# Spreading reciprocal softmax totals on TensorE: one fp32 product against two rounded products of a high and a low part

## The reference, cut to what matters

```python
scores = scores * total_effect
scores = jnp.where(allow, scores, NEG)
attn = jax.nn.softmax(scores, axis=-1)
out = jnp.einsum('bhqk,bhkd->bhqd', attn, v)
```

## Time and profile before

| what | value |
|---|---|
| time before, median of 3 runs | 1689.13 us (1682.05 to 1694.72) |
| time of the profiled execution | 1691.98 us |
| its span, first to last instruction | 1689.0 us |
| its mean granted TensorE clock | 0.953 |
| busy: PE, PEld, DVE, ACT, POOL | 1506.9, 1251.6, 1122.4, 1023.1, 157.9 us |

### The profile page before, as it was taken

How to read it: one execution, slowest core, us unless ns; L and a number is a source line. 1 busy time by engine, 2 the same in 40 slices (tenths; PEclk the granted TensorE clock), 3 DMA queues, 4 the chain that set the end, 5 groups by cost and what they waited for, 6 DMA issues and landing times.

```text
span 1689.0 us, 36801 instructions
## 1 busy us (share of the span) xinstructions
PE 1506.9 (89%) x13056; PEld 1251.6 (74%) x13056; DVE 1122.4 (66%) x3828; ACT 1023.1 (61%) x2674; POOL 157.9 (9%) x107
## 2 busy tenths in 40 slices
PE   4374879999998999999998999999999999988986
PEld 3353668887887888778887878778787878777874
DVE  6576785867766676757857676775857676673221
ACT  1485766676666577666766667666756667674221
POOL 6323110100000010100000010100001010000000
PEclk9786979999998999999999999999999999999998
DMA  5555324656565475646565475656557465566875
GB/s 187 194 187 182 125 101 162 237 177 224 176 212 170 172 251 172 230 170 216 190 207 191 157 244 175 225 177 207 194 178 243 156 234 189 199 224 232 292 270 191
DMA packets 81243, 334.54 MB, mean 198 GB/s; under 512 B 10256, under 2 KB 10256, under 8 KB 64272
## 3 DMA queue, kind: packets, MB, share of 16 engines
q1 hardware_dynamic: 81040, 331.92, 57.3%
HBM read 306.72 MB, written 25.17 MB: 196 GB/s over the span
## 4 chain that ended last, share of the span: by engine, by line
PE 65%; DVE 15%; DMA 8%; issue 5%; ACT 3%; POOL 1%; SPq 1%; DVEq 0%; POOLq 0%; ACTq 0%
PE bank L200 19%; PE bank L201 17%; PE bank L202 17%; PE bank L384 5%; DMA out<-rows 4%; PE bank L398 3%; DVE w_sb L938 3%; DMA w_ring<-w_split 3%; DVE w_sb L950 2%; DVE w_sb L961 2%; PE bank L418 1%; DVE s_sb L926 1%; PE bank L408 1%; DVE c_lo L889 1%; DMA w_split<-w_ring 1%
## 5 line engine op out<-in xcount | busy, mean ns | idle before, releaser
L200 PE MATMUL bank<-xt_hi,w_ring 128*128 128x256 f32 x1024 | 298.4, 291 | 1.9 <-ACT h_sb L721 1.9
L201 PE MATMUL bank<-xt_lo,w_ring 128*128 128x256 f32 x1024 | 291.2, 284 | 0.0
L202 PE MATMUL bank<-xt_hi,w_ring 128*128 128x256 f32 x1024 | 290.8, 284 | 0.0
L200 PE MATMUL bank<-w_ring,h_hi 128*128 128x512 f32 x512 | 219.0, 428 | 23.3 <-DMA w_ring<-w_split 14.7
L721 ACT ACTIVATE h_sb<-bank,b_col 128x256 f32<-128x256 f32 x256 | 106.9, 468 | 212.4 <-DVE h_lo L1027 110.1
L201 PE MATMUL bank<-w_ring,h_hi 128*128 128x512 f32 x512 | 206.4, 403 | 0.0
L384 PE MATMUL bank<-qk_sb 32*32 32x256 f32 (+7 forms) x4096 | 174.3, 298 | 35.8 <-DVE m L926 35.4
L662 ACT ACTIVATE p_sb<-w_sb,nm 128x32 f32<-128x32 f32 (+7 forms) x512 | 206.1, 411 | 0.0
L202 PE MATMUL bank<-w_ring,h_lo 128*128 128x512 f32 x512 | 205.8, 402 | 0.0
L200 PEld LDWEIGHTS bank<-xt_hi,w_ring 128*128 128x128 f32 x1024 | 196.8, 192 | 11.8 <-issue 7.2
L201 PEld LDWEIGHTS bank<-xt_lo,w_ring 128*128 128x128 f32 x1024 | 196.9, 192 | 1.9
(11 more groups left out here) (120 smaller groups left out, 3018.8 us busy)
## 6 DMA issues: line engine op xcount, KB each, us to landing
w_ring<-w_split SPq DMA_DIRECT2D x128, 1024.0 KB, 4.9
w_ring<-w_split SPq DMA_DIRECT2D x256, 512.0 KB, 4.1
w_split<-w_ring SPq DMA_DIRECT2D x32, 512.0 KB, 3.9
x_raw<-x_t SPq DMA_DIRECT2D x16, 512.0 KB, 5.6
c_raw<-ctx_t SPq DMA_DIRECT2D x16, 512.0 KB, 6.2
u_sb<-x_rows SPq DMA_DIRECT2D x16, 512.0 KB, 5.4
ring_raw<-w SPq DMA_DIRECT2D x32, 256.0 KB, 3.0
out<-rows SPq DMA_DIRECT2D x16, 512.0 KB, 6.1
```

What stands on the lines that cost most here:

```text
L200: nc.tensor.matmul(dst, a_hi, b_hi, start=start, stop=False)
L201: nc.tensor.matmul(dst, a_hi, b_lo, start=False, stop=False)
L202: return nc.tensor.matmul(dst, a_lo, b_hi, start=False, stop=stop)
```

## The change

The constant `head_ones_r` is a float32r copy of `head_ones`, made by POOL in its chain of constants. `totals` now makes three more values from the reciprocals: a rounded high part by a copy (128 x 8), a low part by a subtraction (128 x 8), each behind a wait for the last, and one multiplication with `delta` for both parts together, 128 x 512 in place of 128 x 256. `attend` makes two float32r products of 256 columns that add up, in place of one plain fp32 product of 256 columns. Everything else stays as it is.

```diff
+        head_ones_r = tensor("head_ones_r", [P, P], F32R)
...
-        zi_wide = tensor("zi_wide", [P, NB, R])
+        zi_pair = tensor("zi_pair", [P, 2, NB], F32R)
+        zi_wide = tensor("zi_wide", [P, 2, NB, R], F32R)
...
-                nc.tensor.matmul(av_bank[:, S:2 * S], head_ones[:], zi_wide[:].rearrange("p b r -> p (b r)"),
-                                 start=True, stop=True, skip_group_check=True)
+
+                for part in range(2):
+                    nc.tensor.matmul(av_bank[:, S:2 * S], head_ones_r[:], zi_wide[:, part].rearrange("p b r -> p (b r)"),
+                                     start=part == 0, stop=part == 1, skip_group_check=True)
...
                 nc.vector.reciprocal(z2[:, c], z2[:, c]).then_inc(zi2_ok, 1)
-                dve.wait_ge(zi2_ok, NQ * i + c + 1)
+                dve.wait_ge(zi2_ok, 3 * (NQ * i + c) + 1)
+                nc.vector.tensor_copy(zi_pair[:, 0], z2[:, c]).then_inc(zi2_ok, 1)
+                dve.wait_ge(zi2_ok, 3 * (NQ * i + c) + 2)
+                nc.vector.tensor_tensor(zi_pair[:, 1], z2[:, c], zi_pair[:, 0].bitcast(F32),
+                                        ALU.subtract).then_inc(zi2_ok, 1)
+                dve.wait_ge(zi2_ok, 3 * (NQ * i + c) + 3)
                 if c > 0 or not first(i):
                     dve.wait_ge(av_mm, NQ * i + c)
-                nc.vector.tensor_tensor(zi_wide[:], z2[:, c].unsqueeze(2).broadcast_to([P, NB, R]),
-                                        delta[:].unsqueeze(1).broadcast_to([P, NB, R]), ALU.mult).then_inc(wide_ok, 1)
+                parts = zi_pair[:].bitcast(F32).rearrange("p n b -> p (n b)")
+                nc.vector.tensor_tensor(zi_wide[:].rearrange("p n b r -> p (n b) r"),
+                                        parts.unsqueeze(2).broadcast_to([P, 2 * NB, R]),
+                                        delta[:].unsqueeze(1).broadcast_to([P, 2 * NB, R]), ALU.mult).then_inc(wide_ok, 1)
...
+            then(nc.gpsimd.tensor_copy(head_ones_r[:], head_ones[:]))
...
-CONSTS = 4 + 9 + 1 + 12 + 1 + 8
+CONSTS = 4 + 9 + 1 + 12 + 1 + 1 + 8
```

## The result

| | median us (range, runs) | ratio to before, 95% interval |
|---|---|---|
| before | 1685.99 (1679.25 to 1694.72, 17) | |
| after | 1691.19 (1688.96 to 1702.89, 17) | 1.0043 [1.0025, 1.0061] |

A forecast was written before the change was run, and what follows sets the result against it. A PE stretch and a stretch from the store through DVE to `rows_low(0)`, in series, were taken as the bound; 0.35 + 1.5 + 6.8 - 7.8 + 0 = +0.9 us gave a median of 1690 us, range 1679 to 1699.

The forecast's parts named there:

- Two stretches in series: Each turn: a PE stretch, then 24 us from the store to `rows_low(0)` in which PE has room to spare.
- s and d: Per call, s is PE's saving at `attend`, 0.20 us; d is DVE's added time in `totals`, 0.73 us.
- Quarter 3 pays, the others don't: DVE's added time delays `hidden_low(7)` and PE in quarter 3, 6.8 us; quarters 0 to 2 are covered, at nothing.
- eight full and five partial charges: Quarter 3, in front of `add_hidden(7)`: 8 x 0.73 + 5 x 0.2 = 6.8 us.
- POOL's copy at the start: Filling stage: the 128 x 128 copy joins the chain of constants that `inputs_high(0)` waits for, 0.35 us.
- Where the PE saving lands: `attend(3)`, `attend(0)`, `attend(1)` shorten the PE stretch by 0.60 us a turn, 7.8 us; `attend(2)` lengthens the wait for `xt_lo`.
- where the DVE time lands: Quarters 0 to 2 cost nothing; quarter 3 delays `hidden_low(7)`, for which PE waits, 6.8 us in all.
- Rival B: Longer waits at `turn_rows` make the clock fall at six more, 2.0 us each: 1702 us; chance 0.12.
- Rival A: PE bounds everywhere, all its saving counts and DVE's longer work hides: -10.9 us, 1678 us; chance 0.13.
- rival D: At `attend` the second product waits or the switch stays slow, saving only 0.09 us: +5, 1694 us; chance 0.07.
- rival C: DVE's small operations cost more beside ACT and DMA traffic, 1.2 us a call: +8, 1697 us; chance 0.08.
- the 13 places: Starts of `add_hidden(7)` behind `hidden_low(7)`, 320 to 1480 us; PE 0.12 to 0.14 us behind DVE at 8, later at five.

The follow-up runs named there:

- e1: Changed kernel with DVE's `totals` as before, into a float32r tile that both products read, low part left out: 1681.42 us, ratio 0.9968.
- e2: Kernel before with DVE's copy, subtraction and wide multiplication in quarter 3 only, second part unused: 1690.87 us, ratio 1.0028.
- e3: Kernel before with DVE's copy, subtraction and wide multiplication in quarters 0, 1 and 2 only, second part unused: 1688.30 us, ratio 1.0008.
- a2: The changed kernel, same code, measured once more: 1692.72 us, ratio 1.0034 to before.
- f2: Changed kernel with seven overwritten products filling PE's wait ahead of the second half of `turn_rows`: 1695.24 us, ratio 1.0050 to before.
- g1: Changed kernel with POOL's `add_bias` made to wait for `hidden_low(7)` of the same step: 1688.40 us, ratio 1.0009 to before.
- f1: Kernel before with seven overwritten products filling PE's wait ahead of the second half of `turn_rows`: 1690.13 us, ratio 1.0019.

## Why the prediction was right, and where it was off

The forecast was 1690 us, +0.9 us for the change; measured are 1691.19 and +5.2 (by the ratio, +7). That the level came within 1.2 us is partly luck: it was built on a median of three runs, 1689.13, which is 3.1 us above that of the 17, and this made up for most of what the change cost more than the 0.9.

- **Two stretches in series.** Right. PE's own saving counted for 5.4 us (e1) rather than 12.8; 7.4 had been summed for it. (That a turn takes 93 to 98 us was read too narrowly: two of the turns with a jump took 100.9 and 101.2 us before.)
- **s and d.** 0.19 for 0.20 us, 0.67 for 0.73. The two small operations took 0.20 us each, start to start; the 0.10 that would follow from the remark on semaphores in the Trainium skill (VectorE: DVE Perf Modes, The DRAIN you can't avoid) was half of that.
- **Quarter 3 pays, the others don't.** Right. e2 cost 4.7 us where eight full and five partial charges gave 6.8, and e3 1.3 where 0 to 1.5 were summed, mostly for the filling stage. The lower value in e2 fits with d being 0.67 and with more places at a low clock (8 of 11 in its trace), where PE is late by itself.
- **POOL's copy at the start.** 0.29 us of duration; `x_hi` starts at 18.03 instead of 17.68, 0.35 us later, as taken.
- **Where the PE saving lands.** Partly off. The saving of `attend(2)` was to lengthen the wait for `xt_lo`; that grew by 1.0 us from 600 to 1400 us, but the wait in front of `add_hidden(6)` by 3.0. So a turn at full clock became 0.5 us longer rather than 0.1. Why that wait grew so much is open.
- **The step that was off** is "where the DVE time lands". I followed the 0.67 us to the operation behind it and to PE, but not to who runs beside that operation at its new time. `hidden_low(7)` lost its lead over POOL's `add_bias` in some executions, and then 0.7 us became 2.8. That term is missing from the sum. In single executions it was 0 us (after), 5.9 (a2) and, with the filling, 7.8 (f2) of PE's waits. An estimate of its average is 4 to 6 us, from the two ratios of the changed kernel, 1.0043 and 1.0034, against g1's 1.0009, but their intervals overlap.
- **Rival B**, the clock: half seen. The clock is indeed lower in the changed kernel (0.9505 and 0.953 against 0.956), and a fall costs what was taken or somewhat less: turns without a jump took 95.0 us with one and 93.0 to 93.8 without, before, and 93.8 in f1 in the places of those two. f1 doesn't refute the rival, since its new issue waits and longer falls at the jump ate the gain. For the rival speaks that the profiled executions of e1 and g1, with falls at 9 of 11 waits at `turn_rows`, were the longest of their kernels (1688.82 and 1693.88 us, where the medians are 1681.42 and 1688.40). And the two causes are not separate. Behind the collision's waits the clock fell in two of three turns of f2, 5.5 us after `turn_rows`, where no other trace has a fall, and in a2 two falls lasted 6.8 us, where such a fall lasts 3.4 in the others. How much of the excess is the collision and how much clock stays open: over its runs g1 still has a low mean clock, 0.952, with a time like that of before. Rival A fell with e1, rival D with s, rival C with d.

## What to carry to other kernels

When work is added to an engine that seems to have time, ask for each place which wait behind it ends on it; three of four places cost nothing that could be measured here and the fourth nearly all. Then look at what the delayed operation runs beside at its new time: here a two-input operation of DVE on SBUF that came 0.1 to 0.5 us behind a GpSimd operation waited for all of it, in seven of seven cases. One profile each is not enough for a difference of 0.4%: the pair of traces pointed the other way, and the collision showed only in another execution of the same code. And an experiment that removes a cause, as the filling did with the falls, tells little by its total time until the trace shows what else it brought.

## What the runs showed of the hardware that was not expected

- A PE start 0.12 to 0.14 us behind the end of the DVE operation that it needs was a wait here, though no idle time was shown ahead of it. In the profile after, with DVE 0.67 us later, a wait of 0.2 to 0.6 us is shown at 8 of the 13 places; before at none.
- Filling an idle stretch of PE of 2.2 us with 1.6 us of products kept the clock up there, but the falls behind the loop's jump then lasted 6.8 us in all four jumps, where the kernel before had 3.4 in two and 6.8 in two. The mean clock rose from 0.956 to 0.959 and the time rose too, by 0.2% (the interval begins at no change). Why the falls at the jump became longer is not shown. So the mean clock of a run, though it went with its time between runs of one kernel, said little between these kernels.
